# Edge attention of a graph network: who evicts the gathers, who makes the low halves, and how softmax pieces are spread

## The chip, the cores and the metric

The kernel runs on one core of one Trainium2 chip. The metric is the device time of one execution in microseconds (us). The engines are TensorE (PE; its weight loads are shown apart as PEld), VectorE (DVE), ScalarE (ACT) and GpSimd (POOL); SyncE (SP) issues the DMAs.

## The reference, cut to what matters

The network has four residual layers on 128 graphs of 64 nodes with 256 features. The change lies in the third, an attention over 512 edges with 4 heads:

```python
# H is x: 128 graphs x 64 nodes x 256; h = 4 heads, dh = 64
Xq = (H @ W_lin.T).reshape(bt, n, h, dh)
Xv = (H @ W_val.T).reshape(bt, n, h, dh)
e = einsum('behd,hd->beh', leaky_relu(Xq[:, src] + Xq[:, dst], 0.2), a)
e = e + log(A0[src, dst] + EPS)[None, :, None]
m = segment_max(e_t, src); ex = exp(e_t - m[src])          # e_t: edges first
attn = ex / segment_sum(ex, src)[src]
Y = segment_sum(attn[..., None] * Xv[:, dst], src)
out = layernorm(x + Y @ W_out.T)
```

## The kernel before

The kernel is a row of stages, each with one program per engine and a barrier between stages: the first layers, `edge_attention` (scores and softmax weights), then `attention_and_spectral`. The change is in `edge_attention` alone.

**What the stage does.** `xq` holds the query projections of all graphs in SBUF. Matrix products are made exact enough by splitting a float32 operand into a high half, which is the operand rounded to the matmul's format, and a low half, which is the operand less its high half. For each graph a *stack* has the 64 rows of high halves on one half of the partitions and the 64 rows of low halves on the other, so that one matmul with the 0/1 matrix `gather` adds both and sums source and destination rows for all 512 edges. The stages of one graph are:

- `build(j)` on VectorE (L1261 to L1270): the stacks of batch j, which has four graphs: for each of two partition halves a cast of 512 columns (high), a wait for it, a subtraction (low). Three batches of stacks are held (`STACKS`).
- gather on TensorE (L1355 to L1363): two matmuls of 512 columns into one of three PSUM buffers `sc_g` (`GATHERS`). Graph b needs the buffer that graph b-3 had, so it waits until graph b-3 is evicted (`leaked`).
- eviction on ScalarE (L1247): one activation with the leaky slope of 0.2, 128x1024, from PSUM to one of seven buffers `leaky` (`RING`).
- `dots(r)` on TensorE (L1336): the scores of four graphs, after gather b for each b with b % 4 == 2, one batch behind: sixteen matmul instructions.

**Softmax.** Each quarter of the graphs (32 graphs, 8 batches, `PER_Q` and `PER`) has its scores in one of two PSUM banks. VectorE then adds the logarithm of the adjacency and finds segment maxima and sums by scans over the sorted edges. The pieces run in the passes of the next quarter, spread over VectorE's loop over j behind `build(j)`, each queued in order: `maximum(q)` at j % 8 == 2 (sum, two scans, difference), `total(q)` at 4 (scan, product, scan) once ScalarE has done `exponent(q)` behind graph 12 of the quarter, a half of the reciprocal at 5, the other half and `weights(q)` at 6. TensorE's `turn(q)` transposes the weights, ScalarE and VectorE store their two halves (`weights_hi`, `weights_lo`). The last quarter's pieces run behind the loop, with nothing to cover them. Between them stand eight parts of an eigenvector computation for the fourth layer (`ev.part`, placed by `EV_AT`), small operations on 64 partitions; part 3 hands a sum to GpSimd's `inverse_norm`, and part 4 waits for its answer.

GpSimd clears one tensor at the beginning and does `inverse_norm`; otherwise it is idle in this stage.

Of the kernel before, what the change touches and what calls it, by code (L numbers as in the profile page):

```python
# [1197 lines left out]
def edge_attention(nc, sem, c, m, ev, low, xq, acol, attn):  # L1198
# [2 lines left out]

    RING, GATHERS, STACKS, TWO = 7, 3, 3, 2
    with ExitStack() as ctx:
        def sb(name, shape, dt=F32):
            return ctx.enter_context(nc.sbuf_tensor(name, shape, dt))
# [4 lines left out]
        ps_s = [ctx.enter_context(nc.psum_tensor(f"sc_s{i}", [P, E], F32)) for i in range(2)]  # L1212
        ev.place(xq[0:N, 6 * E:8 * E])
        ev_chain, ev_pool, squares, norms = (sem("ev_" + n) for n in ("chain", "pool_chain", "squares", "norms"))
        EV_AT = {8: 0, 11: 1, 15: 2, 16: 3, 19: 4, 23: 5, 24: 6, 27: 7}
        score, top, tops, ex, run, tot = (xq[:, n * E:(n + 1) * E] for n in range(6))
        load, zero, placed, stacked, gathered, leaked, dotted, work, diff, exped, weighed, turned, high, low = (
            sem("sc_" + n) for n in ("load", "zero", "placed", "stack", "gathered", "leaky", "dot", "softmax_chain", "less_maximum",
                                     "exp", "weights", "transposed", "weights_hi", "weights_lo"))
        BATCH = 2 * TWO  # L1220
        with nc.Block() as block:
            @block.sync
# [2 lines left out]

            @block.gpsimd
            def _(pool):
                pool.memset(apad[:, :, :], 0.0).then_inc(zero, 1)
                ev.inverse_norm(nc.gpsimd, Seq(pool, ev_pool), squares).then_inc(norms, 1)

            @block.scalar
            def _(act):
                a = nc.scalar

                def weights_hi(q):
                    act.wait_ge(turned, q + 1)
                    a.activation(attn[0][:, :, q * P:(q + 1) * P], ps_s[q % 2][:, :].rearrange("p (k e) -> p k e", k=EC),
                                 ACT.Copy).then_inc(high, 1)

                def exponent(q):  # L1240
                    act.wait_ge(diff, q + 1)
                    a.activation(ex, top, ACT.Exp).then_inc(exped, 1)
                for b in range(B):
                    act.wait_ge(gathered, b + 1)
                    if b >= RING:
                        act.wait_ge(dotted, (b - RING) // 4 + 1)
                    a.activation(leaky[b % RING][:, :, :], ps_g[b % GATHERS][:, :, :], ACT.Prelu, alpha=SLOPE).then_inc(leaked, 1)  # L1247
                    q, at = b // PER_Q - 1, b % PER_Q
                    if q >= 0 and at == 12:
                        exponent(q)  # L1250
                    if q >= 0 and at == PER_Q - 1:
                        weights_hi(q)
                exponent(QUARTS - 1)
                weights_hi(QUARTS - 1)

            @block.vector
            def _(dve):
                v = nc.vector
                s = Seq(dve, work)

                def build(j):  # L1261
                    if j >= STACKS:
                        dve.wait_ge(gathered, (j - STACKS + 1) * BATCH)
                    for n in range(2):
                        h, o = slice(n * N, (n + 1) * N), slice((1 - n) * N, (2 - n) * N)
                        rows = xq[h, j * TWO * D:(j + 1) * TWO * D].rearrange("p (t d) -> p t d", d=D)
                        hi, lo = stack[j % STACKS][n][h, :, :], stack[j % STACKS][n][o, :, :]
                        v.tensor_copy(hi, rows).then_inc(stacked, 1)
                        dve.wait_ge(stacked, 4 * j + 2 * n + 1)
                        v.tensor_tensor(lo, rows, hi.bitcast(F32), ALU.subtract).then_inc(stacked, 1)  # L1270

                def maximum(q):
                    dve.wait_ge(dotted, (q + 1) * SLOTS)
                    s.after(v.tensor_tensor(score, ps_s[q % 2][:, :], m["log_adj"][:, :], ALU.add))
                    s.after(v.tensor_tensor_scan(top, m["drop_start"][:, :], score, -BIG, ALU.add, ALU.max))
                    s.after(v.tensor_tensor_scan(tops[:, ::-1], m["drop_last"][:, ::-1], top[:, ::-1], -BIG, ALU.add, ALU.max))
                    v.tensor_tensor(top, score, tops, ALU.subtract).then_inc(diff, 1)

                def total(q):
                    dve.wait_ge(exped, q + 1)  # L1280
                    s.after(v.tensor_tensor_scan(run, m["keep_start"][:, :], ex, 0.0, ALU.mult, ALU.add))
                    s.after(v.scalar_tensor_tensor(tops, run, -1.0 / BIG, m["drop_last"][:, :], ALU.mult, ALU.mult))
                    s.after(v.tensor_tensor_scan(tot[:, ::-1], m["keep_last"][:, ::-1], tops[:, ::-1], 0.0, ALU.mult, ALU.add))
# [12 lines left out]
                build(0)  # L1296
                dve.wait_ge(load, 16)
                dve.wait_ge(zero, 1)
                for k in range(C):
                    for half in range(2):  # L1300
                        h = slice(half * DH, (half + 1) * DH)
                        o = 2 * k + half
                        v.tensor_copy(apad[h, k, o:o + 36 * (SLOTS - 1) + 1:36], ac[h, k:k + 1].to_broadcast([DH, SLOTS])).then_inc(placed, 1)
                PER = PER_Q // BATCH
                vectors = Seq(dve, ev_chain)
                for j in range(1, B // BATCH):
                    build(j)
                    q, at = j // PER - 1, j % PER
                    if q >= 0:
                        if at == 2:  # L1310
                            maximum(q)
                        if at == 4:
                            total(q)
                        if at == 5:
                            inverse(q, 0)
                        if at == 6:
                            inverse(q, 1)
                            weights(q)
                    if j % PER == 1 and q >= 1:
                        weights_lo(q - 1)  # L1320
                    if j in EV_AT:
                        ev.part(v, dve, vectors, EV_AT[j], c["ones"][0:N, 0:N], squares, norms)
                weights_lo(QUARTS - 2)
                maximum(QUARTS - 1)
                total(QUARTS - 1)
                inverse(QUARTS - 1, 0)
                inverse(QUARTS - 1, 1)
                weights(QUARTS - 1)
                weights_lo(QUARTS - 1)
                dve.wait_ge(low, QUARTS)  # L1330

            @block.tensor
            def _(pe):
                t = nc.tensor

                def dots(r):  # L1336
                    pe.wait_ge(leaked, 4 * r + 4)
# [1290 lines left out]
```

## Time and profile before

| | |
|---|---|
| three runs | 2022.4, 2024.41, 2024.45 us (median 2024.41) |
| the profiled execution | 2021.84 us, its span 2020.0 us |
| busy in the span | PE 94%, PEld 80%, DVE 75%, ACT 56%, POOL 33% |
| `edge_attention` | from 1573.1 to 1734.1 us of the span |

A row of a timeline is: start in us, duration in us, engine, line, operation, output and inputs, shape, count; in brackets the idle time just ahead of it and what ended it. Several instructions of one kind are merged into one row (x6), whose duration is from the first start to the last end. Names of buffers are given without numbers; `hidB` is also the memory of `xq` and of the softmax's work tensors.

### The profile page before, as it was taken

The page shows a single profiled execution, that of the slowest core. Times are in us where ns is not written, and L with a number is a line of the kernel's source. Part 1 is how long each engine was busy: PE and PEld are TensorE (multiplying, and loading weights), DVE is VectorE, ACT ScalarE, POOL GpSimd, SP SyncE. Part 2 cuts the span into 40 slices and gives each one's busy share as a digit, 9 for nine tenths or more (in the row PEclk, how much of TensorE's full clock was granted, in tenths as well). Part 3 has the DMA queues.
Part 4 walks back from the last instruction along what each step waited for, and adds up shares of the span by engine and source line. Part 5 has one row for each costly group of instructions (what it writes and reads, how often), then busy time and mean ns, then how long its engine had stood idle before and what let it go on. Part 6 is the DMA issues. An engine that isn't in the chain of part 4 may idle for free. (4 is left out here: it accounts for less than half of the span.)

```text
span 2020.0 us, 32199 instructions
## 1 busy us (share of the span) xinstructions
PE 1907.2 (94%) x11545; PEld 1612.8 (80%) x11545; DVE 1519.1 (75%) x3995; ACT 1134.7 (56%) x1755; POOL 659.6 (33%) x1676
## 2 busy tenths in 40 slices
PE   7999999999999999999999989989699899689996
PEld 7888888888899999987788778867599434479895
DVE  6888875676577677888888879868565588889575
ACT  5555555454454544444444467657575698457575
POOL 2444431332333340000000066466443000107675
PEclk9999999999999999999999999989799999899898
DMA  3111001000000000000000043112221000014022
GB/s 117 32 32 64 1 1 42 1 19 24 1 1 1 1 1 1 21 22 0 1 1 1 21 152 105 43 63 84 69 68 63 1 1 1 11 33 131 19 74 84
DMA packets 61534, 71.13 MB, mean 35 GB/s; under 512 B 3767, under 2 KB 55102, under 8 KB 61374
## 3 DMA queue, kind: packets, MB, share of 16 engines
q1 hardware_dynamic: 61374, 69.07, 10.5%
q8 instruction: 91, 1.49, 0.3%
q14 instruction: 69, 0.57, 0.1%
HBM read 43.90 MB, written 25.17 MB: 34 GB/s over the span
## 5 line engine op out<-in xcount | busy, mean ns | idle before, releaser
L2014 ACT ACTIVATE l_gates<-l_acc,l_b 128x512 f32<-128x512 f32 (+1 forms) x408 | 240.0, 620 | 91.4 <-PE l_acc L475 89.5
L473 PE MATMUL l_acc<-l_x_hi,l_w1x_hi 128*128 128x336 f32 (+1 forms) x544 | 187.2, 344 | 2.2 <-ACT l_gates L2014 2.2
L475 PE MATMUL l_acc<-l_x_lo,l_w1x_hi 128*128 128x336 f32 (+1 forms) x544 | 188.3, 346 | 0.0
L474 PE MATMUL l_acc<-l_x_hi,l_w1x_lo 128*128 128x336 f32 (+1 forms) x544 | 188.0, 346 | 0.0
L473 PE MATMUL l_acc<-l_x_hi,l_w0x_hi 128*128 128x512 f32 x464 | 181.1, 390 | 5.0 <-ACT l_gates L2014 5.0
L474 PE MATMUL l_acc<-l_x_hi,l_w0x_lo 128*128 128x512 f32 x464 | 180.6, 389 | 0.0
L475 PE MATMUL l_acc<-l_x_lo,l_w0x_hi 128*128 128x512 f32 x464 | 180.6, 389 | 0.0
L1902 ACT ACTIVATE l_x_hi<-hT 128x512 fp32r<-128x512 f32 (+1 forms) x112 | 82.6, 789 | 165.7 <-PE l_acc L475 165.7
L2021 ACT ACTIVATE l_gates<-l_cell 128x512 f32<-128x512 f32 (+1 forms) x112 | 63.7, 569 | 194.6 <-DVE l_cell L2073 158.7
L244 POOL TENSOR_TENSOR bi_shifted<-bi_shifted 32x126 f32<-32x126 f32 (+61 forms) x62 | 18.0, 290 | 421.2 <-DVE bi_shifted L231 421.2
L1247 ACT ACTIVATE leaky<-sc_g 128x1024 f32<-128x1024 f32 x128 | 121.1, 1031 | 21.8 <-PE sc_g L1361 21.4
L473 PE MATMUL l_acc<-l_h_hi,l_w0h_hi 128*128 128x512 f32 x320 | 126.1, 394 | 5.0 <-DVE l_h_lo L2085 5.0
L475 PE MATMUL l_acc<-l_h_lo,l_w0h_hi 128*128 128x512 f32 x320 | 126.0, 394 | 0.0
L474 PE MATMUL l_acc<-l_h_hi,l_w0h_lo 128*128 128x512 f32 x320 | 125.6, 392 | 0.0
L2201 POOL TENSOR_TENSOR n_tmp<-n_stats 128x4 f32<-128x4 f32 x64 | 13.3, 208 | 328.4 <-DVE n_stats L2189 327.2
L473 PEld LDWEIGHTS l_acc<-l_x_hi,l_w1x_hi 128*128 128x128 f32 x544 | 103.0, 189 | 11.0 <-ACT l_gates L2014 2.5
L2218 ACT ACTIVATE hT<-hT,n_shift,n_rstd 128x256 f32<-128x256 f32 x192 | 99.4, 590 | 21.0 <-POOL n_shift L2213 21.0
L474 PEld LDWEIGHTS l_acc<-l_x_hi,l_w1x_lo 128*128 128x128 f32 x544 | 102.9, 189 | 8.5
L475 PEld LDWEIGHTS l_acc<-l_x_lo,l_w1x_hi 128*128 128x128 f32 x544 | 102.8, 189 | 8.6
L473 PEld LDWEIGHTS l_acc<-l_x_hi,l_w0x_hi 128*128 128x128 f32 x464 | 87.1, 188 | 24.0 <-ACT l_gates L2014 6.2
L2070 DVE TENSOR_TENSOR l_gates<-l_gates 128x512 f32<-128x512 f32 (+1 forms) x72 | 43.9, 610 | 79.4 <-ACT l_gates L2014 77.8
L475 PEld LDWEIGHTS l_acc<-l_x_lo,l_w0x_hi 128*128 128x128 f32 x464 | 87.1, 188 | 18.2
(521 smaller groups left out, 6159.1 us busy)
## 6 DMA issues: line engine op xcount, KB each, us to landing
xin<-in_x_t SPq DMA_DIRECT2D x16, 512.0 KB, 3.6
hidB<-in_x SPq DMA_DIRECT2D x16, 512.0 KB, 5.0
x<-hT SPq DMA_DIRECT2D x16, 512.0 KB, 3.2
hidB<-x SPq DMA_DIRECT2D x16, 512.0 KB, 3.8
x<-hidB SPq DMA_DIRECT2D x16, 512.0 KB, 2.9
attention_residual<-x SPq DMA_DIRECT2D x16, 512.0 KB, 3.9
out_x<-hT SPq DMA_DIRECT2D x16, 512.0 KB, 2.9
l_rawx<-in_wih SPq DMA_DIRECT2D x4, 1024.0 KB, 5.4
```

Of the source, the lines that this page charges most:

```text
L244: s.after(g.tensor_tensor(prod, vb[:, lo:].unsqueeze(1).to_broadcast([self.Q, 2, w]), self.p[k % 2][:, 2:4].unsqueeze(2).to_broadcast([sel ...
L473: t.matmul(out, left[0], right[0], start=start, stop=False)
L474: t.matmul(out, left[1], right[0], start=False, stop=False)
L475: return t.matmul(out, left[0], right[1], start=False, stop=stop)
L1247: a.activation(leaky[b % RING][:, :, :], ps_g[b % GATHERS][:, :, :], ACT.Prelu, alpha=SLOPE).then_inc(leaked, 1)
L1902: i = nc.scalar.activation(as_windows(xs[s % 2][0][:, ch, 0:bg * nw], nw), cols(p, bg, nw, group, k, ch), ACT.Copy)
L2014: i = a.activation(gates[:, j, q, 0:n], acc[:, j, q, 0:n], FUNC[q], bias=b[:, o:o + 1])
L2021: a.activation(tcell[:, j, 0:n], cell[:, j, 0:n], TANH).then_inc(tc, 1)
L2070: v.tensor_tensor(i_, i_, g_, ALU.mult)
L2201: s.add(p.tensor_tensor(apart, even[:, :, 1], odd[:, :, 1], ALU.subtract))
L2218: i = a.activation(rows[:, r, :], rows[:, r, :], ACT.Identity, bias=self.shift[:, g, r:r + 1], scale=self.rstd[:, g, r:r + 1])
```

## The change

Three things are changed in `edge_attention`.

1. The low halves of the stacks are made by GpSimd: VectorE's `build(j)` only makes the two casts. The semaphore `stacked` becomes `stack_hi` and `stack_lo`; TensorE waits for the low halves. GpSimd's `inverse_norm` stands behind its batch 16.
2. Every ninth graph (4, 13, 22, ... 121: fourteen of them) is evicted by VectorE in place of ScalarE, in two instructions: slope times the value, then the maximum of both. `evict(j - 2)` stands behind `build(j)`. `leaked` becomes two semaphores, for each evicting engine one, and TensorE waits for both.
3. The softmax's pieces are cut finer and put later: maximum at j % 8 == 2, difference at 3, total at 5, total of the run and first reciprocal at 6, second reciprocal and weights at 7; ScalarE's exponent stands behind graph 14 of the quarter instead of 12; seven of the eight eigenvector parts are in other passes.

```diff
-    RING, GATHERS, STACKS, TWO = 7, 3, 3, 2
+    RING, GATHERS, STACKS, TWO, EVERY, TURN = 7, 3, 3, 2, 9, 4
+    def on_vector(b):
+        return b % EVERY == TURN
+    def vector_before(b):
+        return sum(on_vector(n) for n in range(b))
...
-        EV_AT = {8: 0, 11: 1, 15: 2, 16: 3, 19: 4, 23: 5, 24: 6, 27: 7}
+        EV_AT, NORM_AT = {9: 0, 12: 1, 15: 2, 16: 3, 17: 4, 20: 5, 24: 6, 25: 7}, 16
...
             @block.gpsimd
-                pool.memset(apad[:, :, :], 0.0).then_inc(zero, 1)
-                ev.inverse_norm(nc.gpsimd, Seq(pool, ev_pool), squares).then_inc(norms, 1)
+                p = nc.gpsimd
+                p.memset(apad[:, :, :], 0.0).then_inc(zero, 1)
+                for j in range(B // BATCH):
+                    for n in range(2):
+                        if j + n:
+                            pool.wait_ge(stack_lo, 2 * j + n)
+                        else:
+                            pool.wait_ge(zero, 1)
+                        pool.wait_ge(stack_hi, 2 * j + n + 1)
+                        hi, lo = halves_of(j, n)
+                        p.tensor_tensor(lo, rows_of(j, n), hi.bitcast(F32), ALU.subtract).then_inc(stack_lo, 1)
+                    if j == NORM_AT:
+                        pool.wait_ge(stack_lo, 2 * j + 2)
+                        ev.inverse_norm(p, Seq(pool, ev_pool), squares).then_inc(norms, 1)
+                        pool.wait_ge(norms, 1)
...
             @block.scalar
                 for b in range(B):
-                    act.wait_ge(gathered, b + 1)
+                    if not on_vector(b):
+                        act.wait_ge(gathered, b + 1)
...
-                    if q >= 0 and at == 12:
+                    if q >= 0 and at == 14:
                         exponent(q)
...
             @block.vector
-                        v.tensor_copy(hi, rows).then_inc(stacked, 1)
-                        dve.wait_ge(stacked, 4 * j + 2 * n + 1)
-                        v.tensor_tensor(lo, rows, hi.bitcast(F32), ALU.subtract).then_inc(stacked, 1)
+                        v.tensor_copy(halves_of(j, n)[0], rows_of(j, n)).then_inc(stack_hi, 1)
+
+                def evict(j):
+                    for b in range(j * BATCH, (j + 1) * BATCH):
+                        if on_vector(b):
+                            dve.wait_ge(gathered, b + 1)
+                            if b >= RING:
+                                dve.wait_ge(dotted, (b - RING) // 4 + 1)
+                            z, to = ps_g[b % GATHERS][:, :, :], leaky[b % RING][:, :, :]
+                            v.tensor_scalar(to, z, SLOPE, None, ALU.mult).then_inc(scaled, 1)
+                            dve.wait_ge(scaled, vector_before(b) + 1)
+                            v.tensor_tensor(to, z, to, ALU.max).then_inc(leaked_dve, 1)
...
                     build(j)
+                    if j >= 2:
+                        evict(j - 2)
+                    if j == PER + 1:
+                        dve.wait_ge(stack_lo, 2 * PER)
                     q, at = j // PER - 1, j % PER
                     if q >= 0:
                         if at == 2:
                             maximum(q)
-                        if at == 4:
+                        if at == 3:
+                            difference(q)
+                        if at == 5:
                             total(q)
-                        if at == 5:
+                        if at == 6:
+                            total_of_run(q)
                             inverse(q, 0)
-                        if at == 6:
+                        if at == 7:
                             inverse(q, 1)
                             weights(q)
...
             @block.tensor
+                def wait_leaked(b):
+                    pe.wait_ge(leaked_act, b - vector_before(b))
+                    if vector_before(b):
+                        pe.wait_ge(leaked_dve, vector_before(b))
...
                     if b % BATCH == 0:
-                        pe.wait_ge(stacked, b + 4)
+                        pe.wait_ge(stack_lo, 2 * (b // BATCH) + 2)
                     if b >= GATHERS:
-                        pe.wait_ge(leaked, b - GATHERS + 1)
+                        wait_leaked(b - GATHERS + 1)
```

## Rows read from the trace of the kernel before

**Rows 1.** The page: busy us of each engine (share of the span), instructions.

```profile
PE 1907.2 (94%) x11545; PEld 1612.8 (80%) x11545; DVE 1519.1 (75%) x3995; ACT 1134.7 (56%) x1755; POOL 659.6 (33%) x1676
```

**Rows 2.** Windows, length, busy us of PE, PEld, DVE, ACT, POOL; clock; DMA.

```profile
1656.00:1666.00 10.00, 9.44 (x55) 3.99 (x58) 9.44 (x21) 9.33 (x12) 0.00 (x0) 1.00 0.00 0
...
1716.00:1726.00 10.00, 2.29 (x18) 0.42 (x16) 6.39 (x7) 2.14 (x3) 0.00 (x0) 0.81 0.00 0
```

**Rows 3.** Waits from 1570 to 1736: us in total, times, the longest.

```profile
PEld sc_g L1361 <- ACT leaky L1247: 44.1, 63, 0.8
...
ACT leaky L1247 <- PE sc_g L1361: 21.4, 27, 6.0
...
DVE stack L1268 <- PE sc_g L1361: 12.0, 7, 2.1
```

**Rows 4.** Timeline of ScalarE through the stage.

```profile
1588.56 3.77 ACT L1247 ACTIVATE leaky<-sc_g 128x1024 f32<-128x1024 f32 x4 [0.60 <-PE sc_g L1361]
1592.92 3.77 ACT L1247 ACTIVATE leaky<-sc_g 128x1024 f32<-128x1024 f32 x4 [0.59 <-PE sc_g L1361]
...
1625.45 1.28 ACT L1242 ACT_TABLE_LOAD   x1
...
1716.40 1.02 ACT L1247 ACTIVATE leaky<-sc_g 128x1024 f32<-128x1024 f32 x1 [0.59 <-PE sc_g L1361]
```

**Rows 5.** Timeline of TensorE over one batch.

```profile
1587.79 1.67 PE L1361 MATMUL sc_g<-e_gather,stack 128*128 128x512 f32 x6
1589.63 0.73 PE L1361 MATMUL sc_g<-e_gather,stack 128*128 128x512 f32 x2 [0.18 <-ACT leaky L1247]
1590.30 1.92 PE L1346 MATMUL sc_s<-leaky,apad 128*32 128x512 f32 x16
1592.15 0.97 PE L1361 MATMUL sc_g<-e_gather,stack 128*128 128x512 f32 x3
```

**Rows 6.** Groups by line and shape, 1570 to 1736: busy us, mean ns | idle before.

```profile
L1270 DVE TENSOR_TENSOR stack<-hidB,stack 64x512 fp32r<-64x512 f32 x64 | 43.9, 686 | 2.2
...
L1268 DVE CAST stack<-hidB 64x512 fp32r<-64x512 f32 x64 | 27.3, 427 | 15.3 <-PE sc_g L1361 12.0 <-PEq L2575 1.8
L1287 DVE RECIPROCAL hidB<-hidB 128x256 f32<-128x256 f32 x8 | 14.0, 1753 | 0.3
...
L1275 DVE TENSOR_TENSOR_SCAN hidB<-e_drop_start,hidB 128x512 f32<-128x512 f32 x4 | 4.9, 1224 | 0.1
```

**Rows 7.** Groups by line and shape, other stages: same columns.

```profile
L1057 DVE COPY hT<-c_hid 128x1024 f32<-128x1024 f32 x16 | 19.6, 1225 | 36.8 <-PE c_hid L475 36.8
...
L783 POOL TENSOR_TENSOR f_lo<-f_full,f_hi 128x512 fp32r<-128x512 f32 x48 | 64.8, 1366 | 33.1 <-DVE f_hi L1026 33.1
```

**Rows 8.** Timelines of GpSimd and VectorE near 1139.

```profile
1139.18 2.48 POOL L729 TENSOR_TENSOR y<-hT,y 128x1024 fp32r<-128x1024 f32 x1 [39.35 <-ACT y L798]
...
1139.44 2.77 DVE L2085 TENSOR_TENSOR l_h_lo<-l_gates,l_h_hi 128x512 fp32r<-128x512 f32 x1
```

**Rows 9.** Timeline at the stage's beginning.

```profile
1573.11 0.77 DVE L1268 CAST stack<-hidB 64x512 fp32r<-64x512 f32 x1 [1.77 <-PEq L2575]
...
1575.82 2.07 PE L1361 MATMUL sc_g<-e_gather,stack 128*128 128x512 f32 x4 [5.75 <-DVE stack L1270]
```

**Rows 10.** Timeline, 1335 to 1346: VectorE beside GpSimd's subtractions.

```profile
1335.91 1.30 POOL L783 TENSOR_TENSOR f_lo<-f_full,f_hi 128x512 fp32r<-128x512 f32 x1 [0.36 <-DVE f_hi L1026]
1336.05 1.29 DVE L1015 BATCH_NORM_STATS2 bn_stats<-hT 128x6 f32<-128x512 f32 x2 [0.21 <-ACT hT L847]
...
1344.78 1.30 POOL L783 TENSOR_TENSOR f_lo<-f_full,f_hi 128x512 fp32r<-128x512 f32 x1 [0.81 <-DVE f_hi L1026]
1345.31 1.06 DVE L1026 CAST f_hi<-f_full 128x512 fp32r<-128x512 f32 x1 [0.60 <-ACT f_full L855]
```

**Rows 11.** Timeline of VectorE: what the first maximum waits for.

```profile
1614.12 0.69 DVE L1274 TENSOR_TENSOR hidB<-sc_s,e_log_adj 128x512 f32<-128x512 f32 x1 [1.42 <-PE sc_s L1346]
```

**Rows 12.** Window of TensorE at the stage's beginning: length, busy, clock, DMA.

```profile
1577.00:1579.00 2.00, 2.00 (x7) 0.52 0.00 0
```

More of the change, by code:

```diff
@@ L1214, in edge_attention, with rows_of, halves_of @@
         ev_chain, ev_pool, squares, norms = (sem("ev_" + n) for n in ("chain", "pool_chain", "squares", "norms"))
-        EV_AT = {8: 0, 11: 1, 15: 2, 16: 3, 19: 4, 23: 5, 24: 6, 27: 7}
+        EV_AT, NORM_AT = {9: 0, 12: 1, 15: 2, 16: 3, 17: 4, 20: 5, 24: 6, 25: 7}, 16
         score, top, tops, ex, run, tot = (xq[:, n * E:(n + 1) * E] for n in range(6))
-        load, zero, placed, stacked, gathered, leaked, dotted, work, diff, exped, weighed, turned, high, low = (
-            sem("sc_" + n) for n in ("load", "zero", "placed", "stack", "gathered", "leaky", "dot", "softmax_chain", "less_maximum",
-                                     "exp", "weights", "transposed", "weights_hi", "weights_lo"))
+        load, zero, placed, stack_hi, stack_lo, gathered, leaked_act, leaked_dve, scaled, dotted, work, diff, exped, weighed, turned, high, low = (
+            sem("sc_" + n) for n in ("load", "zero", "placed", "stack_hi", "stack_lo", "gathered", "leaky_scalar", "leaky_vector", "scaled", "dot",
+                                     "softmax_chain", "less_maximum", "exp", "weights", "transposed", "weights_hi", "weights_lo"))
+        def rows_of(j, n):
+            return xq[n * N:(n + 1) * N, j * TWO * D:(j + 1) * TWO * D].rearrange("p (t d) -> p t d", d=D)
+        def halves_of(j, n):
+            z = stack[j % STACKS][n]
+            return z[n * N:(n + 1) * N, :, :], z[(1 - n) * N:(2 - n) * N, :, :]
         BATCH = 2 * TWO
@@ L1243, in _ @@
                 for b in range(B):
-                    act.wait_ge(gathered, b + 1)
-                    if b >= RING:
-                        act.wait_ge(dotted, (b - RING) // 4 + 1)
-                    a.activation(leaky[b % RING][:, :, :], ps_g[b % GATHERS][:, :, :], ACT.Prelu, alpha=SLOPE).then_inc(leaked, 1)
+                    if not on_vector(b):
+                        act.wait_ge(gathered, b + 1)
+                        if b >= RING:
+                            act.wait_ge(dotted, (b - RING) // 4 + 1)
+                        a.activation(leaky[b % RING][:, :, :], ps_g[b % GATHERS][:, :, :], ACT.Prelu, alpha=SLOPE).then_inc(leaked_act, 1)
                     q, at = b // PER_Q - 1, b % PER_Q
-                    if q >= 0 and at == 12:
+                    if q >= 0 and at == 14:
                         exponent(q)
@@ L1264, in build @@
                     for n in range(2):
-                        h, o = slice(n * N, (n + 1) * N), slice((1 - n) * N, (2 - n) * N)
-                        rows = xq[h, j * TWO * D:(j + 1) * TWO * D].rearrange("p (t d) -> p t d", d=D)
-                        hi, lo = stack[j % STACKS][n][h, :, :], stack[j % STACKS][n][o, :, :]
-                        v.tensor_copy(hi, rows).then_inc(stacked, 1)
-                        dve.wait_ge(stacked, 4 * j + 2 * n + 1)
-                        v.tensor_tensor(lo, rows, hi.bitcast(F32), ALU.subtract).then_inc(stacked, 1)
+                        v.tensor_copy(halves_of(j, n)[0], rows_of(j, n)).then_inc(stack_hi, 1)
[3 more added lines that the diff above has]
+                            dve.wait_ge(gathered, b + 1)
+                            if b >= RING:
+                                dve.wait_ge(dotted, (b - RING) // 4 + 1)
[3 more added lines that the diff above has]
+                            v.tensor_tensor(to, z, to, ALU.max).then_inc(leaked_dve, 1)
                 def maximum(q):
@@ L1275, in maximum, with difference @@
                     s.after(v.tensor_tensor_scan(top, m["drop_start"][:, :], score, -BIG, ALU.add, ALU.max))
+                def difference(q):
                     s.after(v.tensor_tensor_scan(tops[:, ::-1], m["drop_last"][:, ::-1], top[:, ::-1], -BIG, ALU.add, ALU.max))
@@ L1282, in total, with total_of_run @@
                     s.after(v.scalar_tensor_tensor(tops, run, -1.0 / BIG, m["drop_last"][:, :], ALU.mult, ALU.mult))
+                def total_of_run(q):
                     s.after(v.tensor_tensor_scan(tot[:, ::-1], m["keep_last"][:, ::-1], tops[:, ::-1], 0.0, ALU.mult, ALU.add))
@@ L1322, in _ @@
                         ev.part(v, dve, vectors, EV_AT[j], c["ones"][0:N, 0:N], squares, norms)
+                evict(B // BATCH - 2)
+                evict(B // BATCH - 1)
                 weights_lo(QUARTS - 2)
                 maximum(QUARTS - 1)
+                difference(QUARTS - 1)
                 total(QUARTS - 1)
+                total_of_run(QUARTS - 1)
                 inverse(QUARTS - 1, 0)
@@ L1334, in _ @@
                 t = nc.tensor
+                def wait_leaked(b):
+                    pe.wait_ge(leaked_act, b - vector_before(b))
+                    if vector_before(b):
+                        pe.wait_ge(leaked_dve, vector_before(b))
                 def dots(r):
-                    pe.wait_ge(leaked, 4 * r + 4)
+                    wait_leaked(4 * r + 4)
                     q, at = r // SLOTS, r % SLOTS
```

## The prediction, made before the changed kernel was run

> **What bounds the kernel now.** I read the page first: on one core TensorE is busy 94% of the span, VectorE 75%, ScalarE 56%, GpSimd 33% [rows 1]. Such shares are averages, and the change touches one stage of about 160 us, so the views that count are those of 1573 to 1734 us. In the windows of that stage [rows 2] TensorE and VectorE are both at 9.44 of 10 us, TensorE at full clock, and GpSimd does nothing. From 1716 on, TensorE is nearly idle: the last quarter's softmax, a chain on VectorE, which the change leaves in the same order.
>
> A TensorE that looks full is not thereby the limit. The chain that ended last doesn't reach this stage in the part that I read, so I used the waits: TensorE's weight loads wait 44.1 us for ScalarE's evictions, and ScalarE's evictions 21.4 us for TensorE's gathers [rows 3]. Each waits for the other: a ring. ScalarE's timeline shows it: four evictions, 0.6 us idle, four evictions, every 4.37 us [rows 4]. Counted from the stage's first eviction, the group that starts at 1588.56 begins with graph 11, the next with 15: each begins with a graph 4m+3. The ring is
>
> - graph 4m+3 is evicted, 1.02 us for one, and lets go the PSUM buffer that graph 4m+6 needs: 1588.56 + 1.02 = 1589.58;
> - gather 4m+6 starts at 1589.63, the dots behind it at 1590.30, gather 4m+7 at 1592.15, its eviction at 1592.92 [rows 4, 5].
>
> 1.02 + 0.05 + 0.67 + 1.85 + 0.77 = 4.36, the period. From 1588.56 to 1716.40 there are 29 batches: 29 x 4.365 = 126.6, and the remaining 1.2 us is the activation table load of 1.28 us before the first exponent [rows 4]. So before the change VectorE, though busy 94% in the middle, costs this stage nothing, and ScalarE's evictions of 4m+4, 4m+5 and 4m+6 cost nothing either: they fill 3.77 us of 4.37.
>
> **The change, part by part.** *T* is the moment at which graph 4m+3 is gathered; VectorE's pass j = m+3 can begin then. Graph 4m+7 is gathered at T+4.37.
>
> 1. *Evictions taken off ScalarE.* Graphs 4, 13, ... 121: 14 of 128. ScalarE saves 0.91 us each, 13 us in all, but no time of the ring unless the graph is of the form 4m+3. Gain 0. ScalarE's idle time grows.
>
> 2. *Evictions put on VectorE.* A scaling out of PSUM, 128x1024: the nearest row is the copy of that shape and source, 1.225 us. Then a maximum of PSUM and SBUF of the same size. Its bounds are 0.69, a subtraction of half the columns [rows 6], and twice the copy; a subtraction takes 1.34 ns a column and the copy 1.2, so I take the copy's 1.225 again. With the wait between, about 2.49 us against 1.03. What this costs goes by position. Graphs 31, 67 and 103 are of the form 4m+3 and lie in the ring: 2.49 - 1.03 = 1.46 each, 4.4 together, even with VectorE waiting ready. Graphs 4, 40, 76, 112 (4m+4) must be out before gather 4m+7, at T+3.59. VectorE begins its pass at T with two casts (0.42 each [rows 6], about 0.80 together), so it ends at T+3.3: free, with 0.3 to spare. Six gather matmuls take 1.67, the last begun 1.28 after the first, so 0.51 a graph [rows 5]: graphs 13, 49, 85, 121 (4m+5) are needed at T+4.1, and 22, 58, 94 (4m+6), gathered only at T+1.85, at T+4.6 with a little room behind. All of this holds only if VectorE is on time. Before, the stack buffers gave it slack: only seven of its casts waited for a gather at all [rows 3], so it was late in most passes, at no cost; now an eviction is queued behind its softmax pieces, and gather, dots and ScalarE's next graphs wait for it. This is what is late next.
>
> 3. *Low halves on GpSimd.* VectorE loses 64 x 0.686 = 43.9 us and gains 14 x 2.49 = 34.9. GpSimd's nearest row is 1.37 us for 512 columns [rows 7]: 2 x 1.37 = 2.7 per batch, under 4.37, so GpSimd is no bound, and a stack is ready some 5 us ahead. (64 partitions instead of 128; bounds 0.7, VectorE's own row, and 1.37. Taken 1.32.) At the start nothing covers it. Before, the first gather began at 1575.82 behind casts and subtractions in a row; the first cast took 0.77 beside GpSimd's memset [rows 9]. Now: second cast done 1574.3, two subtractions of 1.32, 1577.0: +1.2 us on the path (0.9 if the first doesn't wait for the second cast).
>
> 4. *GpSimd beside VectorE.* Here the trace speaks against the change. A subtraction of two SBUF tensors, 0.69 us alone, took 2.77 when GpSimd's 1024-column subtraction had begun 0.26 earlier: it ended 0.55 after GpSimd did [rows 8]. A cast took 1.06 instead of 0.42, ending 0.29 after GpSimd's [rows 10]. So these wait for the whole GpSimd operation. An operation with one SBUF input doesn't: two batch-norm sums took 1.29, 0.69 each, beside a GpSimd subtraction [rows 10]. Of the softmax, all scans, the difference and both products read two SBUF tensors; the first sum and the reciprocals don't. In a pass without an eviction they come right behind the casts, just when GpSimd works off its 2.6 us. Cost per such piece between 0 and 2.6; I take a wait for each GpSimd operation in turn.
>
> The Trainium skill ("SBUF — State Buffer", Who interferes with whom) says that a VectorE instruction with at most one SBUF input outside the two-port modes doesn't contend with GpSimd. By it the eviction stays at 2.49. Were it wrong for sources in PSUM, an eviction of form 4m+4 would end up to 2.6 us later, four times less 0.3 of room each: some 9 us more.
>
> 5. *Softmax pieces and eigenvector parts spread.* Same instructions. Pieces: maximum 1.99 us, difference 1.87, total 1.99, total of the run with the first reciprocal 3.05, second reciprocal and weights 2.40 (scans 1.22, reciprocals 1.75 [rows 6], products and sums taken like the subtraction, 0.69, with gaps); eigenvector parts 0.9 to 1.9. Two waits still block VectorE: the maximum for the quarter's last dots (1614.12, T+3.7), and the total for the exponent, now behind graph 46 instead of 44 [rows 11]. The table load again delays one batch by 1.2: no change.
>
> **The walk.** Passes 8 to 31, VectorE's lateness carried from one to the next. Pass 9 evicts 31 and does a part: free at T10+3.5. Pass 10: casts to 4.3, maximum's sum to 5.9 (the dots came late too), its scan held by GpSimd to 7.0, end 8.2. Graph 31's batch lasted 4.37+1.46 = 5.83, so pass 11 starts 2.4 late; casts 3.2, difference held twice, 7.8. Pass 12 starts 3.4 late, casts 4.2, eviction of 40 ends at 6.7 instead of 3.60: the ring loses 3.1. In the same way: 49 loses 0.7 (behind the total, which ends at T+7.7), 58 loses 2.6 (behind reciprocals, weights, part 2), 76 loses 3.7 (behind the difference and part 5), 85 0.6, 94 0.9, 112 1.7 (behind the total: 2.8 + 2.49 = 5.3 against 3.6). With 3 x 1.46: 3.1+0.7+2.6+3.7+0.6+0.9+1.7+4.4 = 17.7. The start, 1.2: **19 us**. Nothing gives time back, since the ring has no slack. Without the holding by GpSimd the same walk gives 49 0.7, 58 1.5, 112 1.7, the three 4.4, start 0.9: 9 us.
>
> The profiled execution took 2021.84, of which 2020.0 is span; the median run 2024.41, the lowest 2022.4. 2021.84 + 19 = 2041, 2024.41 + 19 = 2043: I say 2042.
>
> **Rivals.**
> - *VectorE isn't held by GpSimd* beyond the casts: +9, 2033. For it: no row has a scan beside GpSimd. Against: rows 8.
> - *TensorE's clock falls.* After 5.75 us of idling, the stretch from 1577 to 1579 had clock 0.52, its lower level, and the next was at full clock [rows 12]. Stalls of 2.6 to 3.7 us could do the same. At the lower level four gather matmuls took 2.07, so 0.43 each [rows 9]; eight and twice the dots' 1.86 are 7.2 a batch, 2.8 over the ring; with four such stalls +11 more: 2053. Against: the table load's stall left it at full clock.
> - *Faster: the ring opens.* If ScalarE, relieved of one graph, started the next 4m+3 earlier, the batch would go at TensorE's own pace: six gather matmuls 1.67, and it now waits 0.18 before the seventh and pays some 0.28 to restart [rows 5], so 0.46 less in each of 14 batches: -6.4 + 0.9 = -5.5, 2019. It decides if an eviction by ScalarE, and not the gather, is last before graph 4m+3. Against: the 0.6 idle lies just ahead of it [rows 4].
> - *Nothing moves*: VectorE's evictions fit, the three in the ring cost under 1 us: 2023 to 2027.
>
> **How the numbers follow.** Held and late (+12 to +26, 2036 to 2050) 0.58; not held (2029 to 2036) 0.17; clock falls 0.09; nothing moves 0.07; faster 0.09. The range leaves out the last two and the far end of the clock case: 2030 to 2053. A measurement of this kernel tells about 0.2% (4 us) from no change. Slower 0.84, same 0.07, faster 0.09.
>
> **What would show it.** ScalarE's idle before graph 4m+3 stays 0.6 where VectorE is on time; period 4.37 in batches without an eviction; a hole of 1.5 us or more in ScalarE's evictions at graphs 31, 67, 103 and 40, 76, 112; scans of 2.5 us beside GpSimd; GpSimd's subtraction near 1.3; first gather 1.2 later. Wrong if the period falls below 4.37 in any batch, if scans stay at 1.22, or if GpSimd's subtraction takes over 2.1, when it would set the pace.

## The result and the profile after

The kernel after took 2039.48 us (median of four runs, 2038.09 to 2039.94), the one before 2024.34 (four runs of the same chip, 2022.4 to 2024.45): ratio 1.0073, 95% interval 1.0058 to 1.0087, 15.1 us slower. The profiled execution took 2038.09, its span 2036.0.

From the first cast of the stage to the eviction of graph 127, before: 1573.11 to 1716.40, 143.3 us [rows 4, 9]; after: 1573.52 to 1739.84, 166.3. So the stage is 23.0 us longer. The chain on VectorE behind that eviction is unchanged (17.0 us in both). But the stage that follows, from the last `attn_lo` to the end of the span, is 279.1 us instead of 286.6, although nothing in it was edited. 0.4 (earlier stages) + 23.0 - 7.5 = 15.9 of the 16.0 by which the span grew. The prediction had 19 and 0 for the two large terms.

Busy time, from the page (answers to [rows 1]); it tells nearly nothing, TensorE's sum is the same:

```profile
PE 1907.3 (94%) x11545; PEld 1609.0 (79%) x11545; DVE 1524.9 (75%) x3959; ACT 1122.2 (55%) x1741; POOL 750.5 (37%) x1740
```

Waits from 1570 to 1752 (answers to [rows 3]: us in total, times, longest):

```profile
ACT leaky L1276 <- PE sc_g L1418: 56.7, 35, 7.0
...
PE sc_g L1418 <- DVE leaky L1306: 15.8, 9, 2.5
...
DVE stack L1294 <- PE sc_g L1418: 14.7, 6, 3.5
```

TensorE's wait for VectorE's maximum is new, 15.8 us in nine stalls, and ScalarE's wait for gathers has grown from 21.4 to 56.7. VectorE waits for the gathers more than before, so it isn't short of time on average; it is late at certain graphs. Groups by line of the same stretch (answers to [rows 6]: busy us, mean ns of one | idle before):

```profile
L1253 POOL TENSOR_TENSOR stack<-hidB,stack 64x512 fp32r<-64x512 f32 x64 | 90.3, 1411 | 64.6 <-DVE stack L1294 61.8
...
L1294 DVE CAST stack<-hidB 64x512 fp32r<-64x512 f32 x64 | 32.1, 502 | 18.2 <-PE sc_g L1418 14.7 <-PEq L2632 1.8
L1306 DVE TENSOR_TENSOR leaky<-sc_g,leaky 128x1024 f32<-128x1024 f32 x14 | 17.1, 1224 | 0.5
L1304 DVE TENSOR_SCALAR leaky<-sc_g 128x1024 f32<-128x1024 f32 x14 | 17.1, 1224 | 6.0 <-PE sc_g L1418 5.7
...
L1314 DVE TENSOR_TENSOR_SCAN hidB<-e_drop_last,hidB 128x512 f32<-128x512 f32 x4 | 6.8, 1710 | 0.1
```

Both halves of VectorE's eviction take 1.224 us (1.225 was predicted); GpSimd's subtraction 1.41 (1.32); casts 0.50 instead of 0.43 and the scan of L1314 1.71 instead of 1.22, because of GpSimd (experiment 2, without it, has 0.43 and 1.22 again). ScalarE's timeline around the first losses (answers to [rows 4]):

```profile
1604.91 3.77 ACT L1276 ACTIVATE leaky<-sc_g 128x1024 f32<-128x1024 f32 x4 [1.51 <-PE sc_g L1418]
1609.29 3.77 ACT L1276 ACTIVATE leaky<-sc_g 128x1024 f32<-128x1024 f32 x4 [0.60 <-PE sc_g L1418]
1614.11 1.94 ACT L1276 ACTIVATE leaky<-sc_g 128x1024 f32<-128x1024 f32 x2 [1.05 <-PE sc_g L1418]
1617.01 1.02 ACT L1276 ACTIVATE leaky<-sc_g 128x1024 f32<-128x1024 f32 x1 [0.96 <-PE sc_g L1418]
1621.20 3.77 ACT L1276 ACTIVATE leaky<-sc_g 128x1024 f32<-128x1024 f32 x4 [3.17 <-PE sc_g L1418]
1625.57 2.88 ACT L1276 ACTIVATE leaky<-sc_g 128x1024 f32<-128x1024 f32 x3 [0.59 <-PE sc_g L1418]
1631.49 1.03 ACT L1276 ACTIVATE leaky<-sc_g 128x1024 f32<-128x1024 f32 x1 [3.05 <-PE sc_g L1418]
```

The rows start with graphs 23, 27, 32, 34, 35, 39 and 43. From 23 to 27 the period is 4.38 although VectorE evicts graph 22 in between: free. Graph 31 is VectorE's, it begins at 1613.64 (4.35 behind 27), and 35 comes 7.56 later instead of 4.37: 3.19 lost. From 39 to 43, with graph 40 on VectorE, 5.92: 1.55 lost. TensorE's timeline and windows at graph 31 say where 3.19 comes from (windows: length, busy, clock, DMA):

```profile
1616.27 0.70 PE L1418 MATMUL sc_g<-e_gather,stack 128*128 128x512 f32 x2 [1.74 <-DVE leaky L1306]
1616.90 3.60 PE L1403 MATMUL sc_s<-leaky,apad 128*32 128x512 f32 x16
...
1616.00:1618.00 2.00, 1.73 (x10) 0.73 0.00 0
1618.00:1620.00 2.00, 2.00 (x12) 0.50 0.00 0
...
1666.00:1668.00 2.00, 1.54 (x14) 1.00 0.03 8
```

TensorE idled 1.74 us for the maximum of VectorE's eviction; then the granted clock fell to 0.50, its lower level, and the sixteen dots took 3.60 instead of 1.92 [rows 5]: 1.7 on top of the 1.46. The last window is behind the stall of graph 67, as long to the hundredth, where the clock stayed at 1.00:

```profile
1666.45 0.70 PE L1418 MATMUL sc_g<-e_gather,stack 128*128 128x512 f32 x2 [1.74 <-DVE leaky L1306]
```

Why 40 was late shows in the timeline of VectorE, and GpSimd's beside it:

```profile
1622.57 0.88 DVE L1294 CAST stack<-hidB 64x512 fp32r<-64x512 f32 x2
1623.47 2.21 DVE L1314 TENSOR_TENSOR_SCAN hidB<-e_drop_last,hidB 128x512 f32<-128x512 f32 x1
1625.72 1.59 DVE L1315 TENSOR_TENSOR hidB<-hidB 128x512 f32<-128x512 f32 x1
1627.23 0.86 DVE L1294 CAST stack<-hidB 64x512 fp32r<-64x512 f32 x2
1628.13 1.23 DVE L1304 TENSOR_SCALAR leaky<-sc_g 128x1024 f32<-128x1024 f32 x1
...
1623.13 3.63 POOL L1253 TENSOR_TENSOR stack<-hidB,stack 64x512 fp32r<-64x512 f32 x2 [2.65 <-DVE stack L1294]
```

GpSimd's pair ends at 1626.76; VectorE's subtraction of 0.69 us ends at 1627.31, 0.55 behind it, the same 0.55 as in [rows 8]. Scan and subtraction, 1.22 and 0.69 alone, lost 1.9 us to it, and the eviction of 40 stands behind them.

### The profile page after: what moved, and what is told of

Read it like the earlier page. It is cut to its first block and busy times, and to the rows that moved or that the text cites. A ratio compares the mean times of both kernels' runs of the same rounds, so it can differ in the third digit from the quotient of the medians.

```text
span 2036.0 us, 32403 instructions
## 1 busy us (share of the span) xinstructions
PE 1907.3 (94%) x11545; PEld 1609.0 (79%) x11545; DVE 1524.9 (75%) x3959; ACT 1122.2 (55%) x1741; POOL 750.5 (37%) x1740
## 5 line engine op out<-in xcount | busy, mean ns | idle before, releaser
L1276 ACT ACTIVATE leaky<-sc_g 128x1024 f32<-128x1024 f32 x114 | 108.9, 1028 | 56.8 <-PE sc_g L1418 56.7
L2258 POOL TENSOR_TENSOR n_tmp<-n_stats 128x4 f32<-128x4 f32 x64 | 13.3, 208 | 324.1 <-DVE n_stats L2246 323.0
L1253 POOL TENSOR_TENSOR stack<-hidB,stack 64x512 fp32r<-64x512 f32 x64 | 90.3, 1411 | 64.6 <-DVE stack L1294 61.8
L1418 PE MATMUL sc_g<-e_gather,stack 128*128 128x512 f32 x256 | 80.1, 438 | 28.1 <-DVE leaky L1306 15.8
```

The costliest lines, as they stand in the source:

```text
L1253: p.tensor_tensor(lo, rows_of(j, n), hi.bitcast(F32), ALU.subtract).then_inc(stack_lo, 1)
```

## The experiments

All ratios are to the kernel before, run beside them (its medians 2024.44 for experiments 1 to 4, 2024.36 for 5 to 8, 2024.48 for 9 to 11). Its executions lay between 2019.1 and 2026.6; stages are read from one traced execution of each kernel. "Stage" is from first cast to graph 127's eviction (143.3 before), "next stage" from the last `attn_lo` to the end (286.6).

**1. No eviction on VectorE.** From the kernel after:

```diff
-        return b % EVERY == TURN
+        return False
```

> The changed kernel with all 128 evictions on ScalarE again; low halves stay on GpSimd, the softmax stays spread. M is the time from the stage's first cast to the start of the last eviction: 143.3 us before, 166.3 with the change. Theory (the fourteen evictions on VectorE lengthen a ring of eviction, gather and dots; GpSimd only makes VectorE late, and lateness costs nothing without evictions behind it): period 4.37 everywhere, M 144.5 to 145.5, the start alone being late. Rival (stacks come late from GpSimd, or its hold on VectorE is the cost by itself): M over 155, and TensorE waits for the stack's low halves in the middle of the stage.

2024.51 us, ratio 0.9998 (0.9987 to 1.0010). Stage 144.3, period 4.37 throughout but for the batch with the table load (5.62, before 5.60), next stage 287.0. Two rows of the groups show that the holding by GpSimd was there all the same, stronger than in the kernel after:

```profile
L1294 DVE CAST stack<-hidB 64x512 fp32r<-64x512 f32 x64 | 35.8, 560 | 23.1 <-PE sc_g L1418 19.5 <-PEq L2632 1.8 <-DVE hidB L441 0.3
L1314 DVE TENSOR_TENSOR_SCAN hidB<-e_drop_last,hidB 128x512 f32<-128x512 f32 x4 | 7.8, 1954 | 0.1
```

Parts 1 and 3 of the change cost 1.0 us, its start; a late VectorE costs nothing while nobody waits for it. All the rest needs the evictions.

**2. Low halves back on VectorE, evictions kept.** From the kernel after; GpSimd's loop over the batches goes as well, only its `memset` and `inverse_norm` stay:

```diff
-                        v.tensor_copy(halves_of(j, n)[0], rows_of(j, n)).then_inc(stack_hi, 1)
+                        hi, lo = halves_of(j, n)
+                        v.tensor_copy(hi, rows_of(j, n)).then_inc(stack_hi, 1)
+                        dve.wait_ge(stack_hi, 2 * j + n + 1)
+                        v.tensor_tensor(lo, rows_of(j, n), hi.bitcast(F32), ALU.subtract).then_inc(stack_lo, 1)
```

> The changed kernel with the low halves back on VectorE, so GpSimd is idle; fourteen evictions on VectorE stay. Theory: scans return to 1.22 us, none over 1.3, but each build takes 2.3 us instead of 0.9 ahead of the eviction, so even on time an eviction of form 4m+4 ends at T+4.8 against 3.6 and of form 4m+5 at 4.8 against 4.1: M 158 to 172. Rival (the port that GpSimd holds is most of the 23 us): M 148 to 154.

2050.74 us, ratio 1.0134 (1.0119 to 1.0149). Stage 176.4, so +33.1 and 10 more than the change; that is above what was expected (158 to 172). Every scan is back at 1.22 us, so nothing held VectorE; its own 43.9 us of subtractions made it later than the holding did. With the evictions there, GpSimd's part of the change is a gain of 10 us.

**3 and 4. Sixteen evictions, all in the ring or none.** From the kernel after, graphs 3, 11, 19, ... (all of form 4m+3), then graphs 5, 13, 21, ... (none):

```diff
-    RING, GATHERS, STACKS, TWO, EVERY, TURN = 7, 3, 3, 2, 9, 4
+    RING, GATHERS, STACKS, TWO, EVERY, TURN = 7, 3, 3, 2, 8, 3
```

> The changed kernel with every eighth graph (b % 8 == 3, sixteen) on VectorE, all of the form 4m+3. Theory: each costs 1.46 us at least, however punctual VectorE is: 23.4 and the start's 1.0, M 168, and up to 1.7 more for each stall that lets TensorE's clock fall, to 195 at most. Rival (only VectorE's lateness counts, position doesn't): M as in the run with b % 8 == 5, within 4 us.

2048.78 us, ratio 1.0121 (1.0104 to 1.0137), stage 170.6. ScalarE's timeline where VectorE is on time:

```profile
1588.77 3.77 ACT L1276 ACTIVATE leaky<-sc_g 128x1024 f32<-128x1024 f32 x4 [1.50 <-PE sc_g L1418]
...
1599.02 3.77 ACT L1276 ACTIVATE leaky<-sc_g 128x1024 f32<-128x1024 f32 x4 [1.49 <-PE sc_g L1418]
...
1609.28 3.77 ACT L1276 ACTIVATE leaky<-sc_g 128x1024 f32<-128x1024 f32 x4 [1.49 <-PE sc_g L1418]
```

10.26 us for two batches = 2 x 4.37 + 1.52: the price of an eviction in the ring, 1.46 by the prediction, measured.

```diff
-    RING, GATHERS, STACKS, TWO, EVERY, TURN = 7, 3, 3, 2, 9, 4
+    RING, GATHERS, STACKS, TWO, EVERY, TURN = 7, 3, 3, 2, 8, 5
```

> The changed kernel with every eighth graph (b % 8 == 5, sixteen) on VectorE, all of the form 4m+5, none in the ring. Theory: free where VectorE comes on time (pass with no softmax piece ahead), lost only behind difference, total and reciprocals: some 5 us in each of three quarters, M 150 to 160. Where it is on time the period stays 4.37, and it is below 4.37 nowhere. Rival (ScalarE's relief opens the ring): periods below 4.37 in the batches with an eviction on VectorE.

2035.55 us, ratio 1.0055 (1.0040 to 1.0070), stage 156.5. The same view:

```profile
1605.82 3.77 ACT L1276 ACTIVATE leaky<-sc_g 128x1024 f32<-128x1024 f32 x4 [1.49 <-PE sc_g L1418]
1610.18 2.87 ACT L1276 ACTIVATE leaky<-sc_g 128x1024 f32<-128x1024 f32 x3 [0.59 <-PE sc_g L1418]
1614.54 3.77 ACT L1276 ACTIVATE leaky<-sc_g 128x1024 f32<-128x1024 f32 x4 [1.49 <-PE sc_g L1418]
```

4.36 each, with an eviction in every second batch: outside the ring and on time it is free, and gives nothing back (never below 4.36). The 13 us are lost at the start and in the batches in which VectorE comes to its graph late. The same number of the same instructions costs 14 us of stage more in the ring (170.6 against 156.5). That isn't the ring's price alone: sixteen times 1.52 is 24, nearly all of the 27.3 that experiment 3 lost, and the 13 of experiment 4 are lateness, since its graphs also fall into other passes, behind other softmax pieces.

**5 and 6. Where do the 7.5 us of the next stage come from? First, only a delay.** The kernel before, with 13, then 4, reciprocals behind the last `attn_lo`:

```diff
+                for n in range(13):
+                    s.after(v.reciprocal(run[:, 0:E // 2], tot[:, 0:E // 2]))
```

> The kernel before with thirteen more reciprocals in a row at the end of this stage, about 23.3 us in which nothing else runs: the same lateness for the next stage as the change brings, with none of its edits. In the profiles the stage after this one took 286.6 us before and 279.1 with the change. Theory (TensorE's clock in its pauses depends on when they come, not on what the stage before did): the next stage again departs from 286.6, total +15 to +24. Rival (something in the changed stage leaves the next one quicker): 286.6 again and +23.3 in all.

> The same with four more reciprocals, about 7.2 us. Theory: the next stage between 279 and 287 us, not a fixed length, so the total moves by 0 to +8. Rival: 286.6, total +7.2 within 1.

With 23.2 us of delay 2047.8 (ratio 1.0116, 1.0101 to 1.0132), next stage 287.0 without the delay; with 7.1 us 2031.5 (1.0029, 1.0016 to 1.0042), next stage 289.2. Each costs its own length. The idea that the next stage profits from coming later fell.

**7 and 8. Opening the ring in another way.** The kernel before, and the kernel after without VectorE's evictions, each with an eighth `leaky` buffer (lent from the memory of `attention_residual`, idle here) and the dots of a group in two halves, so that less stands between gather 4m+6 and 4m+7. The lent buffer also needs one more wait on ScalarE, and VectorE does a last piece of the softmax in another order behind the loop; neither is shown:

```diff
-                def dots(r):
+                def dots(r, ks=range(C)):
...
                     if b % 4 == 2 and b > 4:
-                        dots(b // 4 - 1)
+                        dots(b // 4 - 1, (0,))
+                    if b % 4 == 3 and b > 4:
+                        dots(b // 4 - 1, (1,))
```

> The kernel before with the dots of a batch cut in two (features 0 to 127 behind the gather with b % 4 == 2, the rest behind the next gather) and an eighth leaky buffer, everything else as it was. Theory (the period is the ring eviction, gather, dots, gather): the ring loses half the dots, 0.93 us, and TensorE's own pace comes next, 8 x 0.256 + 1.86 = 3.9 us, so the period is 3.9 where VectorE keeps up; its load is some 4.1 us a batch in quarters 1 to 3. M, 143.3 before, becomes 131 to 137. Rival (TensorE is the bound already, its 94% taken at face value): M within 2 us of 143.3.

> The same two edits on the changed kernel with all evictions on ScalarE: low halves on GpSimd, softmax spread. Theory: VectorE's load falls to 2.9 us a batch, GpSimd's is 2.8 to 3.6, so the period is 3.9 throughout: 30 x 0.46 = 14 us less than the 144.3 of the run without evictions, M 130 to 132. Rival: GpSimd's hold on VectorE delays casts and GpSimd now bounds the period: M 136 to 144.

2022.59 us (ratio 0.9990, 0.9980 to 1.0000) and 2020.4 (0.9985, 0.9976 to 0.9994). Period 4.245, not the expected 3.9; stage 140.5 and 141.7, where 131 to 137 and 130 to 132 were expected. In the first the interval reaches up to no change. TensorE's timeline of one such batch, of the first of the two:

```profile
1605.03 1.66 PE L1375 MATMUL sc_g<-e_gather,stack 128*128 128x512 f32 x6
...
1607.62 0.73 PE L1375 MATMUL sc_g<-e_gather,stack 128*128 128x512 f32 x2
...
1609.27 1.67 PE L1375 MATMUL sc_g<-e_gather,stack 128*128 128x512 f32 x6
1610.87 1.06 PE L1359 MATMUL sc_s<-leaky,apad 128*32 128x512 f32 x8
1611.87 0.73 PE L1375 MATMUL sc_g<-e_gather,stack 128*128 128x512 f32 x2
1612.52 1.07 PE L1359 MATMUL sc_s<-leaky,apad 128*32 128x512 f32 x8
1613.52 1.19 PE L1375 MATMUL sc_g<-e_gather,stack 128*128 128x512 f32 x4
```

No bracket, so no pause: 1.60 + 1.00 + 0.65 + 1.00 = 4.25. The ring is open and TensorE itself is the limit, 0.12 us under it. The expectation summed gathers and dots at their pace inside a row and left out what the changes between the two cost, four a batch. TensorE had looked full at 9.44 of 10 us [rows 2], and to within 3% it was.

**9 and 10. The queue of TensorE.** A comparison of all traces at the pause where the next stage loses its time. TensorE's timeline of the kernel before, then of the kernel after:

```profile
1801.36 1.87 PE L2516 MATMUL as_y<-hidB,hT 64*64 64x64 f32 x113 [1.72 <-DVE hidB L2443]
1806.63 0.46 PE L2516 MATMUL as_y<-hidB,hT 64*64 64x64 f32 x15 [3.40 <-issue]
```

```profile
1825.26 2.09 PE L2573 MATMUL as_y<-hidB,hT 64*64 64x64 f32 x128 [1.72 <-DVE hidB L2500]
1828.88 0.38 PE L473 MATMUL as_o<-wo_hi,yt 128*128 128x256 f32 x1 [1.52 <-DVE yt L2510]
```

Before, a row of 128 small matmuls is cut behind the 113th by 3.40 us in which TensorE waits for nothing that the profile shows. It is there in the delayed kernels and in those of experiments 1, 7 and 8, and absent in every kernel with evictions on VectorE. These have, in TensorE's queue, waits for two semaphores where the others have one. The page counts 32199 instructions of all engines before, 32267 in experiment 1 and 32403 after, and 91, 91 and 92 packets on the queue named "instruction". SyncE's timeline has the load of x issued just ahead of the cut, the DMA view of 1799 to 1804 what it fills (packets, MB, share of the 16 DMA engines), and the page the queue of the instructions:

```profile
1799.66 0.94 SPq L2304 DMA_DIRECT2D attention_residual<-x  x2
...
q1 hardware_dynamic: 983, 0.99, 59.8%
...
q8 instruction: 91, 1.49, 0.3%
```

So instructions are themselves brought by DMA, and the cut row runs beside a load that uses 59.8% of the DMA engines' time. Test: the kernel before with more waits on TensorE, for a value reached long ago; in the second run only the ones ahead of gathers 104 to 127.

```diff
+                    if r:
+                        pe.wait_ge(leaked, 1)
                     pe.wait_ge(leaked, 4 * r + 4)
...
+                        if b >= 7:
+                            pe.wait_ge(leaked, 1)
                         pe.wait_ge(leaked, b - GATHERS + 1)
```

> The kernel before with 152 waits more on TensorE's queue in this stage (one ahead of the dots of each group but the first, one ahead of each gather from graph 7 on), all for a value that was reached long ago. Where the stage after is shorter (279.1 to 283.5 us instead of 286.6), TensorE's queue held such additional waits, and a stall is missing that the kernel before has at 1806.63: 3.40 us of idle inside a row of 128 small matmuls, ended by nothing that the profile shows, while the DMA engines are filled by the load of attention_residual. Theory: that stall is TensorE's queue waiting for its next instructions, which a DMA brings; more instructions ahead move the place in the program at which they are due to another time. Then the stall at this row is gone, the next stage takes 279 to 284, this stage 143 to 144 as before, the total 3 to 7.5 us less: 2017 to 2021.5. Rival (VectorE's evictions themselves, or the delay of the stage, give the time back): the stall stays, the next stage takes 286 to 289, the total within 2 us of the kernel before.

> The kernel before with 24 such waits only, ahead of gathers 104 to 127. Theory of the instructions' own loading: the place in the program moves by a few instructions, and the row of 128 matmuls is still cut, now some 10 to 24 matmuls earlier than after the 113th, by a stall of about 3.4 us or a little less; the next stage takes 285 to 289, the total within 2 us of the kernel before. Rival (any change of the queue, or the order in time, does it): the stall is gone or remains after the 113th matmul.

With all of them 2019.03 us, ratio 0.9974 (0.9963 to 0.9984), faster than before (seven executions from 2017.2 to 2019.4, of the kernel before seventeen from 2019.1 to 2026.4); the page counts 122 instructions and one packet more. That is 30 fewer than the 152 waits written, and 6 fewer than 24 in the second run; why is not shown, but 30 and 6 are the numbers of gathers among them that already wait for the stacks too. The row is whole again, and the next stage takes 279.7 us:

```profile
1806.33 2.09 PE L2520 MATMUL as_y<-hidB,hT 64*64 64x64 f32 x128 [1.72 <-DVE hidB L2447]
```

The stage itself takes 1.9 us more, since each batch now waits 0.66 where it waited 0.60. With the few waits 2025.38 us, ratio 1.0004 (0.9995 to 1.0013), next stage 284.6:

```profile
1803.96 1.74 PE L2518 MATMUL as_y<-hidB,hT 64*64 64x64 f32 x104 [1.72 <-DVE hidB L2445]
1808.89 0.92 PE L2518 MATMUL as_y<-hidB,hT 64*64 64x64 f32 x24 [3.19 <-issue]
```

18 instructions more by the page, and the cut stands 9 matmuls earlier than before, each of which is a weight load and a matmul: 9 x 2 = 18. The stall sits at a fixed place in TensorE's stream of instructions. 122 more put that place 61 matmuls earlier, behind the 52nd of the row, and there is no stall there. The DMA view shows what changed. Before, the queue q8 brings no packet from 1780 to 1804; one comes in the window 1801.3 to 1807 (the first row), and the cut row goes on at 1806.63. In experiment 9 one came between 1780 and 1800 (the second row), ahead of the load:

```profile
q8 instruction: 1, 0.02, 1.2%
...
q8 instruction: 1, 0.02, 0.4%
```

It is so in all thirteen traces. In the seven with the cut, no such packet of 16 KB comes in the 12 us ahead of the load of x, the next one starts in the load's last 0.7 us (at 1804.01 before, at 1806.40 in experiment 10), and the row goes on 1.2 to 1.6 us after its end. In the six without the cut, one has come 7.8 to 11.7 us before the load starts.

**11. Together.** The kernel of experiment 8 with the same waits on TensorE's queue (there `leaked_act`):

```diff
+                    if r and 0 in ks:
+                        pe.wait_ge(leaked_act, 1)
                     wait_leaked(4 * r + 4)
...
+                        if b >= 7:
+                            pe.wait_ge(leaked_act, 1)
                         wait_leaked(b - GATHERS + 1)
```

> The opened ring with the low halves on GpSimd and no eviction on VectorE (2020.4 us, its stall 3.68 us at the row of 128 small matmuls, next stage 287.8), with the 152 waits more on TensorE's queue. Theory: stall gone, next stage 279 to 284, this stage 141.7 or up to 1 longer, since TensorE has no pause there and each wait may cost it something: total 2013 to 2018. Rival: the next stage stays at 287 to 289, the total at 2020 to 2022.

2016.23 us, ratio 0.9957 (0.9943 to 0.9970), the fastest of all: 8 us under the kernel before. Stage 141.4, next stage 280.4.

## Why the prediction was right, and where it was not

The forecast was 2042, the time 2039.5. Direction and mechanism hold; the closeness is partly luck, for the stage lost 23.0 where 19 was predicted, and 7.5 came back in a stage of which the prediction said nothing. Inside the stage, too, errors offset each other: 6.3 us for the clock and 1.6 of the start were missed, while VectorE's lateness cost 9.4 us where the walk had 13.3.

| term | predicted | measured |
|---|---|---|
| start of the stage | 1.2 | 2.8 |
| 31, 67, 103 (in the ring) | 1.5, 1.5, 1.5 | 3.2, 1.5, 3.1 |
| 40, 49, 58 | 3.1, 0.7, 2.6 | 1.6, 1.1, 3.8 |
| 76, 85, 94, 112 | 3.7, 0.6, 0.9, 1.7 | 4.0, 0, 0, 1.9 |

- *The ring.* Right. Period 4.37 wherever VectorE was on time, never below 4.34; 1.52 for an eviction in the ring (experiment 3), 0 for one outside it (experiment 4), and no gain from what ScalarE was relieved of.
- *VectorE's price.* 2 x 1.224 us, as taken. By the Trainium skill ("SBUF — State Buffer", Who interferes with whom) instructions with at most one SBUF input, outside the two-port modes, don't contend with GpSimd; the trace agrees, the fourteen evictions average 1224 ns each half with GpSimd at work in the same passes.
- *Holding by GpSimd.* Right in kind: the hold again ends 0.55 us behind GpSimd. The scans were at most 2.21 us, not 2.5, and the first scan of the maximum wasn't held in the pass after 31 (GpSimd had finished by then), which is why 40 lost half of what the walk had. Experiment 1 shows that the hold by itself costs nothing.
- *Start.* The first gather came 3.75 us after the first cast instead of 2.71, so 1.0 later where 1.2 was predicted; the other 1.8 were missed. Graph 4 is evicted in the very first passes, and VectorE came to it only at 1584.08, behind six casts that took 6.57 us beside GpSimd. The prediction counted it among the free ones.
- *The clock.* This rival was given 0.09 as a case of its own; it happened as a part of the main case. In the stalls at 31, 58, 76 and 103 (TensorE idle for 1.74, 1.98, 2.51 and 1.74 us) the clock fell, and the gathers and dots behind them took 1.7, 1.6, 1.4 and 1.6 more than at the full clock. That is all that 31 and 103 lost above their terms; 58 and 76 would have lost 2.2 and 2.6 without it, less than the walk had. At 40, 49, 67 and 112 (idle for 1.53, 1.33, 1.74 and 1.81) it did not fall. The rival had asked for stalls of 2.6 to 3.7 us and taken 2.8 each.
- *The next stage.* Taken as unchanged. Experiments 9 and 10 show that more instructions on TensorE's queue take a stall of 3.4 us out of it. The waits that the change itself adds were not tried alone; but the row is whole in all four kernels with evictions on VectorE, and cut in all that add at most 31 waits to that queue. Without that side effect the kernel after would have stood 3.4 to 7.5 us higher, at 2043 to 2047: still in the range.

Open: the stall explains 3.4 of the 7.5 us. The rest goes with the clock in a second pause some 70 us later, with the same wait of 2.37 us in both kernels: in the windows of 10 us from this pause on, the clock averaged 0.62 and 0.69 before, 1.00 and 0.83 after. In experiment 3 it was 0.96, 0.50 and 0.85, as much lost as before, and there the next stage (283.2) is shorter by the stall's 3.4 alone. What decides it was not settled. That the packet of instructions is late because of the load of x is argued from when it comes; the load was not moved. And whose instructions a packet holds no view tells; that they are TensorE's follows only from its waits moving the cut.

## What to carry to other kernels

Where two engines wait for each other, write the ring out and price every moved instruction by its place in it: here sixteen evictions cost 14 us more in the ring than outside, where they still paid for VectorE's lateness. An engine that is late at no cost becomes expensive the moment that something short-lived, like a PSUM buffer, is queued behind its slow work; that, and not its busy share, is what to check before giving it a job. And compare the stages that an edit didn't touch: here one gave back a third of what the edited stage had lost.

## What the runs showed that was not expected

- Waits that are fulfilled already made the kernel 5.4 us faster (experiment 9): 122 more instructions on TensorE's queue removed a 3.4 us stall that lies some 70 us behind the stage with the edit, and 18 shifted it by exactly 9 matmuls. With 122 more a 16 KB packet of instructions came ahead of a load that filled the DMA engines, and not at its end.
- The granted clock fell to 0.50 after TensorE had idled for 1.74 us (graph 31), and stayed at 1.00 after the same stall at 67. In experiment 3, thirteen batches with an eviction in the ring lasted 5.88 to 5.90 us, the ring's price at the full clock, and one, from graph 59, 8.20. Dots of 1.92 us took 3.60 at the lower level.
- Stages that no edit touches began 0.4 to 3.8 us later from one execution to another (first cast at 1573.1 to 1576.9), so comparisons of stages were made between marks inside one trace.
- Changing between gathers and dots costs TensorE time that no row shows as idle: eight gather matmuls and sixteen dots take 4.25 us in four pieces, where the expectation, from the pace inside a row (0.256 for a gather matmul, 1.86 for the sixteen dots), had 3.9.
